# A graph network on one Trainium2 core: group s-1 weighed and summed in slot s instead of s-2 in slot s, and two empty tiles not gathered

## The reference, cut to what matters

```python
h = jnp.maximum(_layernorm(x, axis=-1), 0.0)
x = x + _L0_gnn_ref(...)   # segment_sum of edge_weight * h[src], two linear maps
x = x + _L1_gnn_ref(...)   # dot-product attention, 4 heads, gated skip
x = x + _L2_gnn_ref(...)   # two GATv2 layers, 4 heads and 1 head
x = x + _L3_gnn_ref(...)   # two typed graph transformer layers, 8 heads
# the core of each attention, for every destination node:
smax = jax.ops.segment_max(score, dst, num_segments=n)
ex = jnp.exp(score - smax[dst])
denom = jax.ops.segment_sum(ex, dst, num_segments=n)
out = jax.ops.segment_sum(xl[src] * alpha[:, :, None], dst, num_segments=n)
# the score is q . k in L1 and L3; in GATv2 it is
e = jax.nn.leaky_relu(xl[src] + xr[dst], NEG_SLOPE)
score = jnp.einsum('ehc,hc->eh', e, att)
```

## Time and profile before

| | us |
|---|---|
| median of 3 runs | 6962.94 (6945.1 to 6965.39) |
| the profiled execution | 6951.92 |
| its span, first to last instruction | 6950.0 |
| GpSimd busy | 4755.9 |
| TensorE busy | 4911.1 |
| VectorE busy | 4761.2 |
| ScalarE busy | 1562.0 |

### The profile page before, as it was taken

One profiled execution on the slowest core, in us unless ns is written; L12 is line 12 of the kernel. 1 busy time (PEld: TensorE's weight loads), 2 busy tenths in 40 slices (PEclk: granted clock), 3 DMA queues, 4 the chain that ended last, 5 costly groups with the idle time before them and its releaser, 6 DMA issues. The chain is left out here.

```text
span 6950.0 us, 92236 instructions
## 1 busy us (share of the span) xinstructions
PE 4911.1 (71%) x26631; PEld 4085.5 (59%) x26631; DVE 4761.2 (69%) x14309; ACT 1562.0 (22%) x4929; POOL 4755.9 (68%) x5008
## 2 busy tenths in 40 slices
PE   2655555667766577777688888867888886667766
PEld 2444444556665465565466666656777775566665
DVE  4444443777877577877577777747777874788786
ACT  2433332222222111111112112111222221121121
POOL 3777776777776577777577666627777763777774
PEclk8666666777677788888799889968887886877776
DMA  4444445666666355555455555547766673666664
GB/s 133 165 164 158 159 164 146 204 216 210 214 217 180 125 161 167 166 155 167 121 171 179 167 164 175 168 121 228 242 229 229 231 219 134 215 226 220 223 226 138
DMA packets 408006, 1267.81 MB, mean 182 GB/s; under 512 B 128774, under 2 KB 189958, under 8 KB 321110
## 3 DMA queue, kind: packets, MB, share of 16 engines
q1 hardware_dynamic: 200000, 760.73, 30.7%
q0 software_dynamic: 200240, 496.31, 25.8%
q10 hardware_dynamic: 7270, 4.88, 0.3%
HBM read 1084.56 MB, written 176.98 MB: 182 GB/s over the span
## 5 line engine op out<-in xcount | busy, mean ns | idle before, releaser
L756 POOL DMA_INDIRECT gathered_rows<-table_l,arena x3056 | 2909.3, 952 | 1192.4 <-issue 904.2
L1298 PE MATMUL ps<-weighted_rows,onehot 128*128 128x136 f32 (+2 forms) x8320 | 1527.4, 341 | 573.9 <-DVE acc L1150 568.8
L1298 PEld LDWEIGHTS ps<-weighted_rows,onehot 128*128 128x128 f32 x8320 | 1353.3, 241 | 729.3 <-DVE weighted_rows L1139 334.1
L1260 PEld LDWEIGHTS ps<-dst_side,onehot_t 128*128 128x128 f32 x8320 | 1299.9, 232 | 384.1 <-issue 318.3
L756 POOL DMA_INDIRECT gathered_rows<-table_l,src_rel_edges x1120 | 1063.7, 950 | 603.5 <-issue 328.4
L1260 PE MATMUL ps<-dst_side,onehot_t 128*128 x8320 | 1381.4, 320 | 90.0 <-DVE products L1067 43.8
L1150 DVE TENSOR_TENSOR acc<-acc,ps 128x136 f32 (+2 forms) x4160 | 1185.9, 285 | 178.1 <-PE ps L1298 83.5
L1256 PE MATMUL ps<-gathered_rows,ident 128*128 128x512 f32 x832 | 547.3, 745 | 307.0 <-DMA gathered_rows<-table_l,arena 302.4
L1072 DVE TENSOR_REDUCE scores<-products 128x16 f32<-128x512 f32 (+2 forms) x1040 | 706.5, 679 | 10.0
L879 PE MATMUL ps<-gathered_rows,onehot 128*128 128x128 f32 x1664 | 346.3, 373 | 465.3 <-ACT gathered_rows L816 464.3
L756 POOL DMA_INDIRECT arena<-table_l,src_rel_edges x544 | 516.5, 950 | 180.2 <-issue 160.3
(11 more groups left out here) (322 smaller groups left out, 6029.5 us busy)
## 6 DMA issues: line engine op xcount, KB each, us to landing
onehot_t<-onehots_turned SPq DMA_DIRECT2D x260, 1024.0 KB
onehot<-onehots SPq DMA_DIRECT2D x260, 1024.0 KB
onehots<-onehot SPq DMA_DIRECT2D x52, 1024.0 KB, 6.8
onehots_turned<-onehot_t SPq DMA_DIRECT2D x52, 1024.0 KB, 4.3
table_l<-arena SPq DMA_DIRECT2D x50, 1024.0 KB
gathered_rows<-table_l,arena POOLq DMA_INDIRECT x3056, 2.5
segment_flags_sb<-segment_flags SPq DMA_DIRECT2D x1300, 8.2 KB
arena<-type_mask_rows SPq DMA_DIRECT2D x75, 256.0 KB
```

Source lines behind the costliest of these rows:

```text
L756: pool.indirect_dma_start(out=home(v, t // GC)[:, t % GC, :], out_offset=None, in_=table, in_offset=bass.IndirectOffsetOnAxis(ap=index[:, ...
L1260: ins = nc.tensor.matmul(ps[:, BZ + k, g * P:(g + 1) * P], e.ohT[:, u, t * P:(t + 1) * P], kRows[:, bass.ds(bs[t % 8], D)], start=not gat, ...
L1298: ins = nc.tensor.matmul(ps[:, BP + n % 3, at:at + PW], e.oh[:, u, t, :], exvT[:, t, :], start=True, stop=True)
```

## The change

- Schedule. In slot s the maxima, the exponentials, the weighing and `sums` now all belong to r = s-1; only the additions of units 4 and 5 (tiles 11 to 15) of o = s-2 are late. `dst_rows` 0 to 3 of s are all in slot s, and the scores of s are turned at the start of slot s+1. A pass has one slot less at its end.
- `first` becomes 8 (s+1) + 6 for a block whose last tile is among the first 11 of its group, and 8 (s+2) otherwise, where it was 8 (s+2) + 7 (first 8) and 8 (s+3) + 1.
- Block registers of the sums are loaded 5 and 11 at a time instead of 8 and 8.
- The two empty tiles are not gathered, in all six passes, and the numbers that the semaphores wait for follow.
- The order inside a GAT pair sum (identity product first) stays.

```diff
+LACK = NT - NT_MAX
+ON_TIME = SUMMED[3][1]
+def rows_wanted(s, j, q):
+    return 64 * (q + 1) - (16 * LACK if s == NG - 1 and j == J - 1 else 0)
...
-            for t in range(GT):
+            for t in range(min(GT, NT_MAX - s * GT)):
...
     ScalarE, slot:
                 after.act(act, x)
-                after.act(act, x + 1)
                 if cur:
                     keep_column(s, u, q)
-                after.act(act, x + 2)
-                after.act(act, x + 3)
+                after.act(act, x + 1)
                 if chain:
                     open_scale(s - 1, 1 - u)
-                after.act(act, x + 4)
+                    exps(s - 1)
+                after.act(act, x + 2)
                 if chain:
-                    exps(s - 1)
-                after.act(act, x + 5)
+                    exp_columns(s - 1)
+                for h in range(3, 7):
+                    after.act(act, x + h)
                 if cur:
                     keep_linear(s, w)
-                after.act(act, x + 6)
-                if chain:
-                    exp_columns(s - 1)
...
     VectorE, slot as it now stands:
+                if late:
+                    bo = blocks_of(o, ON_TIME, GT - ON_TIME)
+                    unit_of_adds(o, 4, ON_TIME, bo)
                 if chain:
                     scan_tiles(r, v, rq)
+                if late:
+                    unit_of_adds(o, 5, ON_TIME, bo)
                 if chain:
                     turn_ends(r)
+                after.dve(dve, x)
                 after.dve(dve, x + 1)
                 if chain:
                     chain_forward(r, v)
                 if cur:
                     product(s, w, qw, 0)
                 if chain:
                     chain_backward(r, v)
                     hand_back_ends(r)
+                    open_drop(r)
+                    max_forward(r, v)
+                    max_backward(r, v)
+                    less_maximum(r)
+                if cur:
+                    score(s, 0)
                 after.dve(dve, x + 2)
                 if chain:
+                    e.excol_ready.wait(dve, a_no, r + 1)
+                    last_maxima(r)
+                    for j in range(J):
+                        weigh(r, (w - 1) % buffers, j)
+                    br = blocks_of(r, 0, ON_TIME)
+                    rescale(r, v, br[0])
                 after.dve(dve, x + 3)
                 if cur:
                     product(s, w, qw, 1)
                     score(s, 1)
+                if chain:
+                    unit_of_adds(r, 0, 0, br)
                 after.dve(dve, x + 4)
                 if chain:
+                    unit_of_adds(r, 1, 0, br)
                 after.dve(dve, x + 5)
                 if cur:
                     product(s, w, qw, 2)
                     score(s, 2)
+                if chain:
+                    unit_of_adds(r, 2, 0, br)
+                    unit_of_adds(r, 3, 0, br)
                 after.dve(dve, x + 6)
                 if cur:
                     product(s, w, qw, 3)
                     score(s, 3)
...
     TensorE, slot as it now stands:
+                if cur:
+                    bs = blocks_of(s, 0)
+                if chain:
+                    turn_scores(r)
                 after.pe(pe, x)
+                if cur:
+                    e.oht_here[u].wait(pe, a_no, 16 * (q + 1))
+                    dst_rows(s, w, qw, 0, bs)
+                after.pe(pe, x + 1)
+                if chain:
+                    spread_drop(r)
+                after.pe(pe, x + 2)
+                if chain:
+                    turn_back(r)
+                if cur:
+                    dst_rows(s, w, qw, 1, bs)
+                after.pe(pe, x + 3)
+                if chain:
+                    e.oh_here[v].wait(pe, a_no, 16 * (rq + 1))
+                    for n in range(3):
+                        sums(r, v, n)
                 if cur:
                     bs = blocks_of(s, 8)
+                after.pe(pe, x + 4)
                 if chain:
+                    sums(r, v, 3)
+                after.pe(pe, x + 5)
                 if cur:
                     dst_rows(s, w, qw, 2, bs)
+                if chain:
+                    sums(r, v, 4)
+                    sums(r, v, 5)
+                after.pe(pe, x + 6)
                 if cur:
                     dst_rows(s, w, qw, 3, bs)
                 after.pe(pe, x + 7)
...
-        return HOOKS * (s + 2) + 7 if t < 8 else HOOKS * (s + 3) + 1
+        return HOOKS * (s + 1) + 6 if t < ON_TIME else HOOKS * (s + 2)
```

More of the change, by code:

```diff
@@ L51, with rows_signals, in_pass @@
 AR = 13184
+def rows_wanted(s, j, q):
+    return 64 * (q + 1) - (16 * LACK if s == NG - 1 and j == J - 1 else 0)
+def rows_signals(sem, name, buffers):
+    def in_pass(v, j):
+        return 64 * len(range(v, NG, buffers)) - (16 * LACK if (NG - 1) % buffers == v and j == J - 1 else 0)
+    return [[Signal(sem(f"{name}_{v}{j}"), in_pass(v, j)) for j in range(J)] for v in range(buffers)]
 def bc(ap, n):
@@ L1047, in _ @@
             slot(NG, NG % ways, NG // ways, cur=False)
-            slot(NG + 1, (NG + 1) % ways, (NG + 1) // ways, cur=False, chain=False)
-            for x in range(HOOKS * (NG + 2), after.end):
+            for x in range(HOOKS * (NG + 1), after.end):
                 after.act(act, x)
@@ L1192, in slot @@
                     chain_backward(r, v)
-                if chain:
                     hand_back_ends(r)
+                    open_drop(r)
[4 more added lines that the diff above has]
+                    score(s, 0)
                 after.dve(dve, x + 2)
                 if chain:
-                    open_drop(r)
-                if cur:
-                    score(s, 0)
-                if weighs:
-                    for t in range(3):
-                        add(p, t, bp[t])
+                    e.excol_ready.wait(dve, a_no, r + 1)
[4 more added lines that the diff above has]
+                    rescale(r, v, br[0])
                 after.dve(dve, x + 3)
@@ L1235, in _ @@
             for s in range(ways):
-                slot(s, s, 0, chain=s > 0, weighs=s > 1, late=s > 2)
+                slot(s, s, 0, chain=s > 0, late=s > 1)
             turns(slot, ways, NG, ways)
-            for n in range(3):
-                slot(NG + n, (NG + n) % ways, (NG + n) // ways, cur=False, chain=n < 1, weighs=n < 2)
-            for x in range(HOOKS * (NG + 3), after.end):
+            slot(NG, NG % ways, NG // ways, cur=False)
+            slot(NG + 1, (NG + 1) % ways, (NG + 1) // ways, cur=False, chain=False)
+            for x in range(HOOKS * (NG + 2), after.end):
                 after.dve(dve, x)
@@ L1249, in dst_rows @@
                 if gat:
-                    here[v][j].wait(pe, here_no, 64 * (qv + 1))
+                    here[v][j].wait(pe, here_no, rows_wanted(s, j, qv))
                 if not (static(s, 1) and j < 2):
@@ L1302, in blocks_of, with slot @@
                 return row_places(nc, e, kRows, GT * s + first, 8)
-            def slot(s, w, qw, cur=True, chain=True, weighs=True, ahead=True):
-                r, p = s - 1, s - 2
-                u, pq = two(*place(w, qw, ways, -2))
-                wn, qn = place(w, qw, ways, 1)
+            def slot(s, w, qw, cur=True, chain=True):
+                r = s - 1
+                u, q = two(w, qw)
+                v, rq = two(*place(w, qw, ways, -1))
                 x = HOOKS * s
+                if cur:
+                    bs = blocks_of(s, 0)
+                if chain:
+                    turn_scores(r)
@@ L1310, in slot @@
                 after.pe(pe, x)
-                if weighs:
-                    e.oh_here[u].wait(pe, a_no, 16 * (pq + 1))
+                if cur:
[9 more added lines that the diff above has]
+                    dst_rows(s, w, qw, 1, bs)
@@ L1313, in slot @@
+                after.pe(pe, x + 3)
[3 more added lines that the diff above has]
+                        sums(r, v, n)
                 if cur:
                     bs = blocks_of(s, 8)
-                if weighs:
-                    sums(p, u, 0)
-                after.pe(pe, x + 1)
-                if weighs:
-                    sums(p, u, 1)
-                    sums(p, u, 2)
-                after.pe(pe, x + 2)
+                after.pe(pe, x + 4)
@@ L1331, in slot @@
                     dst_rows(s, w, qw, 3, bs)
-                after.pe(pe, x + 5)
-                after.pe(pe, x + 6)
-                if weighs:
-                    sums(p, u, 4)
-                    sums(p, u, 5)
-                if chain:
-                    turn_back(r)
-                if cur and ahead:
-                    un, un_q = two(wn, qn)
-                    e.oht_here[un].wait(pe, a_no, 16 * (un_q + 1))
-                    bn = blocks_of(s + 1, 0)
-                    dst_rows(s + 1, wn, qn, 0, bn)
@@ L1344, in slot @@
-                after.pe(pe, x + 7)
-                if cur:
-                    turn_scores(s)
```

(15 more changed lines are left out.)

65 lines of the change are left out of this document (14 added, 51 removed).

## The result

The changed kernel takes 7462.0 us, the median of 4 runs (7459.5 to 7470.2), beside 6956.9 us for the kernel before (4 runs, 6945.1 to 6965.4): a ratio of 1.0729, 95% interval 1.0709 to 1.0750. The forecast was 7560 with a range of 7130 to 7880.

What follows compares the result with a forecast made beforehand. GpSimd's unbroken gathers were taken as the bound, giving way to a longer slot chain: 724 (slots) + 14 (first slots) - 85 (drain) - 40 (lag) - 3 = +610 on the profiled execution, so 7560 us, range 7130 to 7880.

Steps and rivals of the forecast that it cites:

- here the order turns against itself: GAT slot: pair sum 2 stands behind sums unit 3, which awaits an addition; 2.8 us, product 2 at 14.35.
- the prediction's GAT chain: One GAT slot as a chain between VectorE and TensorE at its upper clock level, 20.4 us before any epilogue.
- The epilogue: Per-block epilogue steps on top of the chain: 2.0, 1.8, 4.6, 4.4, 2.4 us a slot in passes 1 to 5.
- the sum of 18.3 + 2.4 + 1.5 us: Pass 5 slot: chain outside GAT 18.3, epilogue 2.4 and lower clock 1.5, giving 22.2 us.
- the eleven behind the weighings: VectorE's register loads before the rescale: hidden in the chain; if not, some 1.2 us a slot, +300 us.
- I keep the present clocks: TensorE's granted clocks by pass stay 0.76, 0.86, 0.90, 0.83, 0.77; a further 140 us only in the upper bound.
- the rival of the chain at full clock: TensorE's short waits needn't lower its clock: slots 20.3 to 24.95 us, about 7220 us; chance 0.20.
- The 1.5 us a slot that I took for the clock: Cost of TensorE's lower clock level on its share of the chain: 1.25 to 1.5 us a slot by pass.
- The drain: End of each attention pass: one slot less, 33.3 us to some 16, -17 in each of five passes, -85.
- the gaps between passes some 17 us shorter: Sign expected in the profile after: GpSimd's idle gaps at pass boundaries shrink by some 17 us.
- the lag hidden in my baseline: Passes 3 and 4: consumers already lag the gathers by the buffers between them, -40 us against the slot figures.
- twelve gathers fewer are 15 us: Skipped gathers at 1.25 us each, 15 us, but free where GpSimd no longer sets the pace; L0 keeps 2.5.

Runs made afterwards that it cites:

- e3: The changed kernel with TensorE's pair sums 2 and 3 moved ahead of the units of sums that wait for additions; 6971.8 us, ratio 1.0013.
- e13: The changed kernel with all sixteen register loads of a group behind its weighings, none at the next slot's top; 7279.4 us, ratio 1.0481.
- e8: e3 with every block's hooks in pass 4 counted from a slot's first hook; 6933.5 us, ratio 0.9968.
- e9: e8 with TensorE's first hook of a slot moved behind pair sum 0; 6916.6 us, ratio 0.9942.
- e1: The kernel before with only the two empty tiles' gathers left out, schedule unchanged; 6942.8 us, ratio 0.9970.
- e2: The changed kernel with every tile gathered again, so the new schedule alone; 7473.1 us, ratio 1.0735.
- e11: e9 with pair sum 2 moved once more, ahead of unit 2 of the sums; 6886.6 us, ratio 0.9892.
- e12: e11 with all sixteen register loads of a group behind its weighings; 6823.7 us, ratio 0.9801.
- e4: The changed kernel with the late additions' five register loads moved ahead of product 3 of the slot before; 7468.7 us, ratio 1.0722.

## Why the prediction was right

**The mechanism.** The step that decided was "here the order turns against itself": sums behind additions and pair sums 2 and 3 behind those sums. The trace has waits where the prediction put them, 1.81 us ahead of product 2 (predicted 2.8 less 0.9 of additions) and 1.96 ahead of product 3 (predicted 2.75), and e3 shows the order to be the cause: both pair sums out of it, and 490 of 505 us are gone. The bound moved as foreseen, from GpSimd to the chain between VectorE and TensorE.

One half of it looks different in the changed kernel than the prediction says. Ahead of unit 5 TensorE does wait for an addition, 1.34 us in nearly every slot, 308 us in the five stretches of the table. Ahead of unit 3 it hardly does, 89 us in all and 8 in pass 2: pair sum 1 ran at the lower clock level in 50 of the 52 slots of pass 2, and TensorE is through with units 0 to 2 only when unit 0 is added. In e13, where the five loads are gone, lighter slots have pair sum 1 at the upper level, and there the predicted wait stands open (TensorE, then VectorE):

```profile
3097.80 0.93 PE L1295 MATMUL ps<-weighted_rows,onehot 128*128 128x136 f32 x6 [1.71 <-DVE acc L1160]
3098.57 1.02 PE L1253 MATMUL ps<-gathered_rows,ident 128*128 128x512 f32 x2
```

```profile
3100.52 0.69 DVE L1075 SCALAR_TENSOR_TENSOR products<-ps,vectors 128x512 f32<-128x512 f32 x1 [1.81 <-PE ps L1257]
```

Product 2 waits 1.81 us in both kernels, so the slow pair sum 1 only fills a wait that the order makes anyway. This slot of e13 is the prediction's GAT chain link by link: counted from the end of score 3, product 0 comes at 2.9, the weighing at 6.6, product 2 at 14.4, product 3 at 19.4 and the end at 20.8 us, where 2.85, 6.6, 14.35, 19.0 and 20.4 stood.

**The sizes**, from the same slot lengths as above:

| pass | 1 | 2 | 3 | 4 | 5 |
|---|---|---|---|---|---|
| slot predicted | 21.8 | 23.7 | 26.2 | 24.1 | 22.2 |
| slot measured | 21.9 | 23.0 | 24.7 | 26.2 | 21.0 |
| 47 slots against before, predicted | 82 | 172 | 216 | 155 | 99 |
| measured | 85 | 141 | 146 | 255 | 41 |

Together 668 us where 724 were forecast. Pass 3 was sized 70 too high and pass 4 100 too low. The epilogue was the term that I had said could be half as large: in pass 4, 4.4 us a slot was taken, with key, value and query products only where they meet short waits, and every second slot there is a heavy one of 31 us. On top of e3's order, e8 and e9 take 46 us off pass 4 by hooks alone. In pass 5 the sum of 18.3 + 2.4 + 1.5 us was 1.2 us too much; which of the terms was, no run tells.

**A term that was missed.** The five register loads at the top of each slot. The prediction weighed the eleven behind the weighings and rightly had them hidden (the rescaling at 2870.78 follows the last weighing at once, where the earlier trace rows had 0.9 us of idle), but did not ask where the other five would stand. By e13 their place costs 183 us. This is not a share beside e3's 490: together they would be more than the 505, since both lie on one chain. The sum came out near by luck in part: the rest was sized too high by somewhat more. e13 is the kernel that the prediction priced, with no loads in the open: it takes 7279.4 us, 327 over the kernel before it was measured beside, where I had 610. Its slots, over whole passes, are 20.3, 22.4, 24.6, 25.3 and 20.6 us, some 500 us in place of 724.

The Trainium skill, TensorE: Matmul & The Clock Gate, "Architectural detail: the array is 16× 32×32, not 1× 128×128", gives VectorE a strict queue of eight. That register loads run on while the queued operations are at work is my reading; the page doesn't speak of them. The trace agrees with this reading: with four weighings ahead the loads behind them cost nothing, eleven or sixteen. Where no run of work is ahead of them, before product 3 or at a slot's top, five of them stand open at 1.2 and 0.87 us.

**The clock.** "I keep the present clocks" held: 0.78, 0.87, 0.90, 0.76 and 0.79 for 0.76, 0.86, 0.90, 0.83 and 0.77. Only pass 4 fell. The changed kernel lies 242 us above the rival of the chain at full clock (7220) and 98 below the forecast. But e13, the kernel that both had priced, comes to 7279.4 with the clock of pass 2 at 0.91, nearer to the rival. The 1.5 us a slot that I took for the clock was too much at least in a GAT slot, where pair sum 1 at the lower level falls into a wait.

**The drain** was right in its size. Last score and last block's first step at the end of pass 1, VectorE, as the earlier trace rows:

```profile
2314.36 0.69 DVE L1082 TENSOR_REDUCE scores<-products 128x16 f32<-128x512 f32 x1
...
2331.16 1.66 DVE L1160 TENSOR_TENSOR acc<-acc,ps 128x132 f32 x5 [1.58 <-issue]
2332.85 0.17 DVE L1766 TENSOR_SCALAR row_scalars<-acc 128x4 f32<-128x4 f32 x1
```

18.5 us for 33.3, so -15 where -17 stood; 1.58 of it is "issue" where again five register loads stand. By the last addition, the five passes give 15, 16, 21, 29 and 19 us, 100 where -85 stood. But the sign that I named for it, "the gaps between passes some 17 us shorter", was wrong: GpSimd's five gaps grew from 393.3 to 441.5 us. GpSimd is now further ahead of the consumers when its pass ends, and the gap holds that lead too: from its last gather to the last score it is 37 us in pass 1 and 67 in pass 2, where it was 11 and 13. The passes' own lengths give 513 us, the slots 668, so 155 come off, where the prediction had 114. The drain is 100 of them. Another 65 (40 predicted) are the lag hidden in my baseline: from score to score the slots of passes 3 and 4 before were 22.5 and 21.3 us long, not 21.6 and 20.8. L0 gives 7, and some 17 us the other way were not traced.

**The gathers.** That twelve gathers fewer are 15 us, but free where GpSimd no longer sets the pace, agrees with e1's time and with the profile of e2; e2's time can't tell it.

**The signs.** Gathers waiting for weighings and passes above 1100 us were seen, and a wait ahead of the weighing (0.63 us in the slot above, at 2868.26, for 0.5). Taken together, TensorE's waits for additions tell nothing, 441 us in 390 waits where the kernel before had 569 in 400; by unit they do, as said above.

## What to carry to other kernels

When a pipeline loses a stage, write the in-order streams side by side and look for a producer that stands behind a consumer's result: here two lines of TensorE's order were worth 490 us, and with them put right one stage less cost almost nothing (ratio 1.0013). Scalar loads on a compute engine have a place just as instructions have; put them behind a run of long operations without waits, never ahead of the instruction on which the other engine waits. Cost an epilogue by the link that its largest product stands ahead of, slot by slot, not as a mean.

## What the runs showed of the hardware

Five register loads on VectorE took no time behind four weighings of 0.6 us, 0.87 us at a slot's top and 1.2 to 1.26 us ahead of a product. Moving the same five from the slot's top to behind the weighings gave 183 us in the changed kernel (e13) and 63 us from e11 to e12, by what else bound the slots.

TensorE's granted clock did not follow how good a schedule is. Pass 2 had 0.87 in the changed kernel, 0.83 in e3, which is 134 us shorter there, 0.81 in e4 and 0.91 in e13. In pass 2 of e4, each of 18 stands of 3.1 to 3.3 us was followed by a pair sum at the lower level, and 28 of 33 stands of 1.5 us by one at the upper.
